# Identity products that nobody reads, in the last stage of a two-layer gated cross-attention kernel

## The chip, the cores and the metric

The kernel runs on one core of a Trainium2 chip. The metric is the device time of one execution, in microseconds. Before the change three runs gave 2161.19, 2162.99 and 2169.70 us, so the median is 2162.99 us.

## What is computed

The reference runs two layers over 32 sequences of 100 tokens with 128 features and a context of 1444 rows each. Layer 0 is a gated cross-attention block and a gated feed-forward with quantised weights. Layer 1 is a gated masked cross-attention with 16 heads of 8 and a gated feed-forward part, which is what the last stage of the kernel computes:

```python
attn_out = _attention(src, Wq, bq, Wk, bk, Wv, bv, Wo, bo)   # 16 heads over 100 tokens
x = _ln(src + attn_out, ln1_g, ln1_b)
ff = _moe(x, gW, gb, W1, b1, W2, b2)                         # 8 experts, width 256, top 2
return _ln(x + ff, ln2_g, ln2_b)
```

Every expert is computed for every token, and its hidden values are multiplied by the token's gate, which is zero for experts outside the top two. All of it is in fp32.

## The kernel before

The program has a setup and three stages, each in a block of its own: the engines meet at the border between two blocks. `stage_a` does layer 0, `stage_b` the masked cross-attention of layer 1, and `stage_c` (line 1646) all that follows. The change is in `stage_c`, in the stream of TensorE.

`stage_c` works on 8 units of 4 sequences (`UNITS`, `GROUP`), 400 tokens each (`TG`). The self-attention of a unit is cut into 8 pieces of half a sequence's heads, so there are 64 pieces (`PIECES`), and the order on every engine is written out as a loop over pieces k, one slot for each. In a slot TensorE issues, in this order:

- `scores(k + 1)` (line 2090): four heads' scores in each of two row groups of 32, into banks 0 and 1. They wait for `sub_ready`, VectorE's subtraction of the row maxima of piece k (lines 2316 and 2320), which frees these banks.
- `turn_pieces(k)` (line 2099): eight transposes of the exponentials. They wait for ScalarE's `exponent(k)` (line 1920).
- by the slot's place s in the unit's eight: a back-transpose of attended values (`back`, 2139), a turn of tokens (`turn0`, `turn1`, `turn2`, all through line 2038), or the query projection (2072).
- for slots from 22 on, `hidden(2n)` and `expert(2n - 2)` (lines 2191 and 2202), where n = k - 22.
- `weigh(k)` (line 2111): 16 heads' probabilities against values, eight matmuls of 32 columns of weights. It waits for ScalarE's copy of the transposed piece (`keep`, line 1926).
- again by s: the attended projection of the next unit (`attended`, 2053), the outer projection or values (through `project`, 2043), keys (2068), the gate's matmuls (2043).
- for slots from 22 on, `hidden(2n + 1)` and `expert(2n - 1)`.

The experts run 22 slots behind (`LAG`), because a unit's gates need the end of its attention. So slots 0 to 21 hold no expert work, slots 22 to 63 hold both, and 22 more steps (`TAIL`) hold the experts alone. Each `hidden` and `expert` is one matmul of 400 columns with 128 x 128 weights; GpSimd multiplies its hidden values by the gates in between (`weigh_hidden`, 1814), from a broadcast copy `G` that SyncE loads through DRAM (`spread_gates`, 1728).

Ahead of the slots stands a lead-in for unit 0: the attended projection, VectorE's entry with the moments of a layer norm (`enter`, 2304), GpSimd's reciprocal root, ScalarE's normalisation (1883), the turn, then keys, queries, values and the first scores, each waiting for ScalarE's copy of the one before (lines 1896, 1902, 1908).

PSUM bank 7 (`SUM_BANK`) holds the running sum of the experts; its first matmul is issued in slot 23 with `start=True`. At the end of `stage_a` there is already a helper `keep_busy` (line 863) of the same form as the new one, on bank 4.

Of the kernel before, what the change touches and what calls it, by code (L numbers as in the profile page):

```python
# [23 lines left out]
D = 128  # L24
# [5 lines left out]
TG = GROUP * T  # L30
# [1615 lines left out]
def stage_c(nc, t, x1, att, gates, w1, w2, out):  # L1646

    with ExitStack() as ctx:
# [6 lines left out]
        psum, K, tanhs, ident = t.psum, t.K, t.tanhs, t.ident  # L1655
        w, col, row, bank, tok_bank = t.w, t.col, t.row, t.bank, t.tok_bank
# [46 lines left out]
        OUT_BANK, MISC, HIDDEN_BANK, SUM_BANK = 4, 5, 6, 7  # L1703
# [10 lines left out]
        def sum_bank(u):  # L1714

            return OUT_BANK if u == LAST - 1 else SUM_BANK
# [316 lines left out]
        def _(pe):  # L2033
            mm = nc.tensor.matmul

            def turn(src, signal):
                for j in range(GROUP):
                    last = nc.tensor.transpose(bank(MISC, D, T, j * T), src[:, j, :], ident[0:T, 0:T])  # L2038
                last.then_inc(signal, 1)

            def project(b, lhsT, rhs, signal, width=D):
                for j in range(GROUP):
                    last = mm(bank(b, T, width, j * width), lhsT[:, t.ts_(j)], rhs, start=True, stop=True)  # L2043
                last.then_inc(signal, 1)

            def attended(u):
                pe.wait_ge(t.sem["ain_ready"], u + 1)
                if u == 1:
                    pe.wait_ge(sem["fv_ready"], 1)
                if u >= 2:  # L2050
                    pe.wait_ge(sem["fu_ready"], (u - 1) * GROUP)
                for j in range(GROUP):
                    m = mm(bank(MISC, T, D, j * D), AIN[:, u % 2, t.ts_(j)], w("xo"), start=True, stop=True)  # L2053
                m.then_inc(sem["attx_psum"], 1)

            def turn0(u):
                pe.wait_ge(normed[0], u + 1)
                if u == 1:
                    pe.wait_ge(sem["fu_ready"], 1)
                if u >= 2:  # L2060
                    pe.wait_ge(sem["r_used"], u - 1)
                turn(H[:, u % 3], turned[0])

            def keys(u):
                pe.wait_ge(tokT[0], u + 1)
                if u:
                    pe.wait_ge(sem["fu_ready"], (u - 1) * GROUP + 2)
                mm(bank(MISC, D, TG), w("fk"), HT[:, :], start=True, stop=True).then_inc(sem["fk_psum"], 1)  # L2068

            def queries(u):  # L2070
                pe.wait_ge(sem["fk_ready"], u + 1)
                mm(bank(MISC, D, TG), w("fq"), HT[:, :], start=True, stop=True).then_inc(sem["fq_psum"], 1)  # L2072

            def values(u):
                pe.wait_ge(sem["fq_ready"], u + 1)
                if u:
                    pe.wait_ge(sem["fu_ready"], (u - 1) * GROUP + 3)
                project(MISC, HT, w("fv"), sem["fv_psum"])

            def scores(k):  # L2080
                m, c = divmod(k, 2)
                u, j = divmod(m, GROUP)
                pe.wait_ge(sem["kbd_ready"], m + 1)
                pe.wait_ge(sem["fq_ready"], u + 1)
                if k:
                    pe.wait_ge(sem["sub_ready"], k)
                for b in range(2):
                    r = 2 * c + b
                    dims = slice(32 * r, 32 * r + 32)
                    x_ = mm(bank(b, T, TG), FQ[dims, u % 2, t.ts_(j)], KBD[dims, u % 2, j, :],  # L2090
                            start=True, stop=True, tile_position=(32 * r, 0))
                x_.then_inc(sem["fs_psum"], 1)

            def turn_pieces(k):
                pe.wait_ge(sem["fe_ready"], k + 1)
                if k:
                    pe.wait_ge(sem["fpT_ready"], k)
                for a in range(8):
                    x_ = nc.tensor.transpose(bank(2 + a // 4, T, T, (a % 4) * T), P[:, k % 2, t.ts_(a)], ident[0:T, 0:T])  # L2099
                x_.then_inc(sem["fpT_psum"], 1)  # L2100

            def weigh(k):
                m, c = divmod(k, 2)
                u, j = divmod(m, GROUP)
                pe.wait_ge(sem["fpT_ready"], k + 1)
                pe.wait_ge(sem["fv_ready"], u + 1)
                if m and not c:
                    pe.wait_ge(sem["os_ready"], m)
                for a in range(8):
                    r, q = a % 4, 2 * c + a // 4  # L2110
                    x_ = mm(psum[32 * r:32 * r + 32, OUT_BANK, q * T:(q + 1) * T], VS[:, u % 2, j, 8 * c + a, :],  # L2111
                            PT[:, k % 2, a // 4, t.ts_(r)], start=True, stop=True, tile_position=(0, 32 * r), skip_group_check=True)
                x_.then_inc(sem["fo_psum"], 1)
# [28 lines left out]
            def turn1(u):  # L2142
                pe.wait_ge(sem["fu_ready"], (u + 1) * GROUP)
                if u + 2 < UNITS:
                    pe.wait_ge(sem["x_ready"], u + 3)
                turn(U[:, u % 2], turned[1])

            def outer(u):
                pe.wait_ge(tokT[1], u + 1)
                pe.wait_ge(sem["fu_ready"], min((u + 1) * GROUP + 1, BATCH))  # L2150
                project(MISC, OT, w("fo"), sem["wo_psum"])

            def turn2(u):
                pe.wait_ge(sem["y_ready"], u + 1)
                if u + 2 < UNITS:
                    pe.wait_ge(sem["fv_ready"], u + 3)
                elif u < LAST:
                    pe.wait_ge(sem["fu_ready"], LAST * GROUP + 3)
                else:
                    pe.wait_ge(sem["u_ready"], LAST - 2)  # L2160
                turn(Y[:, u], turned[2])
# [32 lines left out]
            def expert(c):  # L2194
                u, w_ = divmod(c, 2 * EXPERTS)
                b = bank(sum_bank(u), D, TG)
                if w_ == 0 and u:
                    pe.wait_ge(sem["yT_ready"], u)
                if w_ == 0 and u == LAST - 1:
                    pe.wait_ge(sem["os_ready"], BATCH)  # L2200
                pe.wait_ge(sem["moe_g_ready"], c + 1)
                mm(b, W2[:, w_ * D:(w_ + 1) * D], HE[:, c // 2 % 2, c % 2, :], start=(w_ == 0), stop=False,  # L2202
                   skip_group_check=True).then_inc(sem["moe_y_psum"], 1)
                if w_ == 2 * EXPERTS - 1:
                    pe.wait_ge(g_loaded[0], 32 * (u + 1))
                    mm(b, t.B2[:, :], WT[:, u % 2, :], start=False, stop=True, skip_group_check=True).then_inc(sem["yT_psum"], 1)

            attended(0)
            turn0(0)
            keys(0)  # L2210
            queries(0)
            values(0)
            scores(0)
            for k in range(PIECES):
                b, s = divmod(k, SLOTS)
                n = k - LAG
                if k + 1 < PIECES:
                    scores(k + 1)
                turn_pieces(k)
                if s % 2 == 0 and k:  # L2220
                    back(k // 2 - 1)
                if s == 1 and b:
                    turn1(b - 1)
                if s == 3 and b < LAST:
                    turn0(b + 1)
                if s == 5 and b < LAST:
                    queries(b + 1)
                if s == 7 and b:
                    turn2(b - 1)
                if n == 0:  # L2230
                    pe.wait_ge(sem["big_loaded"], 32)
                if n >= 0:
                    hidden(2 * n)
                if n >= 1:
                    expert(2 * n - 2)
                weigh(k)
                if s == 0 and b < LAST:
                    attended(b + 1)
                if s == 2 and b:
                    outer(b - 1)  # L2240
                if s == 4 and b < LAST:
                    keys(b + 1)
                if s == 5 and b >= 4:
                    turn_experts(b - 4)
                if s == 6 and b < LAST:
                    values(b + 1)
                if s == 7 and b:
                    gate(b - 1)
                if n >= 0:
                    hidden(2 * n + 1)  # L2250
                if n >= 1:
                    expert(2 * n - 1)
# [262 lines left out]
```

## Time and profile before

| what | value |
|---|---|
| median of 3 runs | 2162.99 us |
| profiled execution | 2172.06 us, span 2170.3 us |
| TensorE busy | 1935.4 us, 89% of the span |
| VectorE, ScalarE, GpSimd busy | 68%, 61%, 31% |
| mean granted clock of TensorE | 0.924 |
| last stage | from 1675.46 us to the end of the span |

A granted clock of 1.00 is 2.4 GHz and 0.50 is 1.2 GHz; a figure in between is a stretch with both. The profile has one row for a group of equal instructions that follow each other: start, time from the first start to the last end, engine, line, the tensors written and read, shapes, count. An fp32 matmul leaves two records, so a single product of 400 columns reads x2. "Idle before" in brackets is the wait of that engine and what ended it.

### The profile page before, as it was taken

What the parts mean: (1) busy time and instruction counts of PE and PEld (TensorE: products, weight loads), DVE (VectorE), ACT (ScalarE), POOL (GpSimd) and SP (SyncE); (2) the same over time, 40 slices, a digit from 0 to 9 for tenths busy, and PEclk for the clock granted to TensorE, in tenths of its full rate; (3) what the DMA queues carried; (4) which work ended last, traced back from release to release, by engine and by line L of the source; (5) the groups of instructions that cost most, each with busy time, mean ns of one, the idle gap of its engine ahead of it and who ended that gap; (6) DMA issues with size and microseconds to landing.
All of it is one profiled execution on the core that took longest, in us unless ns stands there. A gap on an engine that the chain in (4) does not pass through costs nothing. (4 is left out here: it accounts for less than half of the span.)

```text
span 2170.3 us, 42902 instructions
## 1 busy us (share of the span) xinstructions
PE 1935.4 (89%) x16792; PEld 1224.2 (56%) x16792; DVE 1481.8 (68%) x3509; ACT 1321.2 (61%) x2169; POOL 670.7 (31%) x605
## 2 busy tenths in 40 slices
PE   3669999766899999999999999999998899999997
PEld 2536766444465656656566565665655455555553
DVE  4844666785778787777877778777783456577541
ACT  2635677586166666666666666666776345666643
POOL 1410223321422131322313223131221323566576
PEclk9879999877599999999999999999999557999998
DMA  5025555001232332323323232232332102221222
GB/s 157 1 69 189 168 186 172 26 27 47 89 106 82 114 119 72 131 82 114 108 84 131 81 115 97 95 131 68 124 105 75 24 12 45 48 41 36 36 70 42
DMA packets 126293, 190.74 MB, mean 88 GB/s; under 512 B 42018, under 2 KB 99466, under 8 KB 125710
## 3 DMA queue, kind: packets, MB, share of 16 engines
q1 hardware_dynamic: 126094, 188.01, 27.9%
q8 instruction: 134, 2.20, 0.4%
q14 instruction: 65, 0.53, 0.1%
HBM read 104.84 MB, written 11.76 MB: 54 GB/s over the span
## 5 line engine op out<-in xcount | busy, mean ns | idle before, releaser
L1607 DVE TENSOR_REDUCE b_part_max<-psum 128x1 f32<-128x482 f32 (+3 forms) x1248 | 738.6, 650 | 200.8 <-PE psum L1493 186.0
L1413 ACT ACTIVATE b_PT<-psum 128x800 f32<-128x800 f32 x768 | 614.9, 836 | 335.4 <-PE psum L1512 329.5
L1493 PE MATMUL psum<-b_KH,b_QBD 64*128 64x482 f32 (+1 forms) x1152 | 416.2, 441 | 37.4 <-DVE b_part_max L1607 35.0
L1512 PE MATMUL psum<-b_QS,b_KS 64*128 64x200 f32 x3072 | 436.7, 288 | 0.3 <-ACT b_PT L1413 0.3
L1512 PEld LDWEIGHTS psum<-b_QS,b_KS 64*128 64x128 f32 x3072 | 346.2, 187 | 15.2 <-issue 10.5
L1528 PE MATMUL psum<-b_PT,b_V 128*32 128x200 f32 x6144 | 341.4, 339 | 0.3 <-ACT b_PT L1413 0.3
L1493 PEld LDWEIGHTS psum<-b_KH,b_QBD 64*128 64x128 f32 x1152 | 194.1, 189 | 182.1 <-DVE b_part_max L1607 115.7
L1338 POOL TENSOR_TENSOR b_KL<-b_KF,b_KH 128x1444 fp32r<-128x1444 f32 x32 | 106.9, 3340 | 589.7 <-PE psum L1512 566.5
L1528 PEld LDWEIGHTS psum<-b_PT,b_V 128*32 128x32 f32 x6144 | 159.9, 109 | 144.6 <-ACT b_PT L1413 78.7
L1814 POOL TENSOR_TENSOR c_HE<-c_HE,c_G 128x400 f32<-128x400 f32 x128 | 131.5, 1032 | 112.6 <-ACT c_HE L1960 106.0
L426 POOL TENSOR_TENSOR a_rs<-a_ve,a_half 100x4 f32<-100x4 f32 x48 | 48.5, 1011 | 312.6 <-DVE a_ve L918 312.5
L2316 DVE TENSOR_REDUCE c_peak<-psum 100x8 f32<-100x800 f32 x64 | 63.2, 987 | 96.0 <-PE psum L2090 95.9
L1480 PE MATMUL psum<-W,b_CT 128*128 128x128 f32 (+1 forms) x768 | 117.7, 293 | 7.0
L1960 ACT ACTIVATE c_HE<-psum,C 128x400 f32<-128x400 f32 x128 | 75.5, 593 | 75.9 <-PE psum L2191 74.7
L2202 PE MATMUL psum<-c_HE,c_W 128*128 128x400 f32 x256 | 110.1, 513 | 9.7 <-POOL c_HE L1814 9.3
L1480 PEld LDWEIGHTS psum<-W,b_CT 128*128 128x128 f32 (+1 forms) x768 | 92.7, 188 | 35.5 <-DVE b_part_max L1607 31.6
L1926 ACT COPY c_PT<-psum 100x800 f32<-100x800 f32 x64 | 52.8, 825 | 96.6 <-PE psum L2099 96.6
L2191 PE MATMUL psum<-c_YT,c_W 128*128 128x400 f32 x256 | 110.4, 513 | 0.0
L1476 PE MATMUL psum<-b_CT,W 128*128 128x482 f32 (+1 forms) x192 | 103.0, 623 | 6.5 <-DVE b_QF L1589 2.5
L959 DVE TENSOR_SCALAR_CACHE_REDUCE a_nz<-psum 1x422 bf16<-1x422 f32 (+1 forms) x96 | 59.8, 643 | 67.4 <-PE psum L716 67.3
L716 PE MATMUL psum<-a_CT,a_RT 128*100 128x422 f32 (+1 forms) x192 | 93.0, 596 | 8.3 <-ACT a_P L524 7.1
L741 PE MATMUL psum<-a_P,a_CN 128*128 128x100 f32 (+1 forms) x768 | 98.9, 281 | 0.0
(280 smaller groups left out, 2988.2 us busy)
## 6 DMA issues: line engine op xcount, KB each, us to landing
b_KS<-b_KH SPq DMA_DIRECT2D x64, 722.0 KB
a_CT<-in_ctxt SPq DMA_DIRECT2D x32, 722.0 KB, 5.6
b_CT<-in_ctxt SPq DMA_DIRECT2D x32, 722.0 KB, 4.3
b_KS<-b_KL SPq DMA_DIRECT2D x32, 722.0 KB
a_CN<-in_ctxn SPq DMA_DIRECT2D x32, 704.0 KB
c_G<-gates_scratch SPq DMA_DIRECT2D x16, 800.0 KB, 4.3
att_scratch<-b_AO SPq DMA_DIRECT2D x32, 200.0 KB, 5.8
b_MB<-in_mask SPq DMA_DIRECT2D x32, 180.5 KB, 4.4
```

The lines of the kernel that those rows point to most:

```text
L741: x_ = mm(bank(7, D, T, TG), CN[0:rows, m % 3, k, :], PTA[0:rows, m % 2, k, :], start=(k == 0), stop=(k == KT - 1))
L1338: pl.tensor_tensor(KL[:, :], KF[:, 0:S], KH[:, j % 2, :].bitcast(F32), ALU.subtract).then_inc(sem["kl_ready"], 1)
L1413: nc.scalar.activation(PT[:, kt % 2, 2 * a:2 * a + 2, :], psum[:, 2 * a:2 * a + 2, 0:TG], ACT.Exp).then_inc(sem["pt_ready"], 1)
L1476: m = mm(bank(b, D, size), w("xkT"), CT[:, j % 2, c:c + size], start=True, stop=True)
L1480: m = mm(bank(b, rows, D, (k % 4) * D), CT[:, j % 2, k * D:k * D + rows], w("xvT"), start=True, stop=True)
L1493: m = mm(bank(b, D, size), QBD[rows, j % 2, tile * D:(tile + 1) * D], KH[rows, j % 2, at_:at_ + size], start=True, stop=True)
L1512: m = mm(bank(p, D, 2 * T, (s % 2) * 2 * T), KS[rows, j % 2, s, kt * D:(kt + 1) * D], QS[rows, j % 2, s * 2 * T:(s + 1) * 2 * T], start=Tr ...
L1528: m = mm(psum[32 * r:32 * r + 32, 6, b * 2 * T:(b + 1) * 2 * T], V[:, j % 2, kt, 4 * b + r, :], PT[:, kt % 2, 2 * b + r // 2, (r % 2) * 2 ...
L1607: v.tensor_reduce(part_max[0:rows, q, c:c + 1], bank(b, rows, CHUNKS[c][1]), AX.X, ALU.max)\
L1814: pl.tensor_tensor(h, h, G[:, e, :], ALU.mult).then_inc(sem["moe_g_ready"], 1)
L2191: mm(bank(hidden_bank(c), D, TG), W1[:, w_ * D:(w_ + 1) * D], YT[:, u, :], start=True, stop=True).then_inc(sem["moe_h_psum"], 1)
L2202: mm(b, W2[:, w_ * D:(w_ + 1) * D], HE[:, c // 2 % 2, c % 2, :], start=(w_ == 0), stop=False, skip_group_check=True).then_inc(sem["moe_y_p ...
```

## The change

A helper `keep_busy(count)` issues `count` matmuls: the 128 x 128 identity as weights, the first 400 columns of the weight pack `W` as the moving operand, into bank 7. It waits for nothing and signals nobody, and nobody reads the result. In the lead-in there are six products ahead of `attended(0)`, three ahead of `turn0(0)`, and two ahead of each of `keys(0)`, `queries(0)`, `values(0)` and `scores(0)`. In each slot with n < 0 (slots 0 to 21) two stand ahead of `turn_pieces(k)` and two ahead of `weigh(k)`. That is 17 + 88 = 105 products.

```diff
--- before.py
+++ after.py
@@ -2205,17 +2205,30 @@
                     pe.wait_ge(g_loaded[0], 32 * (u + 1))
                     mm(b, t.B2[:, :], WT[:, u % 2, :], start=False, stop=True, skip_group_check=True).then_inc(sem["yT_psum"], 1)
 
+            def keep_busy(count):
+
+                for _ in range(count):
+                    mm(bank(SUM_BANK, D, TG), ident, t.W[:, 0:TG], start=True, stop=True)
+
+            keep_busy(6)
             attended(0)
+            keep_busy(3)
             turn0(0)
+            keep_busy(2)
             keys(0)
+            keep_busy(2)
             queries(0)
+            keep_busy(2)
             values(0)
+            keep_busy(2)
             scores(0)
             for k in range(PIECES):
                 b, s = divmod(k, SLOTS)
                 n = k - LAG
                 if k + 1 < PIECES:
                     scores(k + 1)
+                if n < 0:
+                    keep_busy(2)
                 turn_pieces(k)
                 if s % 2 == 0 and k:
                     back(k // 2 - 1)
@@ -2233,6 +2246,8 @@
                     hidden(2 * n)
                 if n >= 1:
                     expert(2 * n - 2)
+                if n < 0:
+                    keep_busy(2)
                 weigh(k)
                 if s == 0 and b < LAST:
                     attended(b + 1)
```

The change moves no other instruction. On TensorE, in the lead-in of the last stage (W is the weight pack, K holds the identity, c_H, c_HT, c_P and c_PT are the normalised tokens, the same turned, the exponentials and the same turned), the order was:

```order
L2053 MATMUL psum<-W,AIN 100x128 x4
L2038 MATMUL psum<-K,c_H 128x100 x4
L2068 MATMUL psum<-c_HT,W 128x400
L2072 MATMUL psum<-c_HT,W 128x400
L2043 MATMUL psum<-W,c_HT 100x128 x4
L2090 MATMUL psum<-c_KBD,c_FQ 100x400 x4
L2099 MATMUL psum<-K,c_P 100x100 x8
L2111 MATMUL psum<-c_PT,c_VS 32x100 x8
```

and is now, with line 2211 the new product:

```order
L2211 MATMUL psum<-W,K 128x400 x6
L2053 MATMUL psum<-W,AIN 100x128 x4
L2211 MATMUL psum<-W,K 128x400 x3
L2038 MATMUL psum<-K,c_H 128x100 x4
L2211 MATMUL psum<-W,K 128x400 x2
L2068 MATMUL psum<-c_HT,W 128x400
L2211 MATMUL psum<-W,K 128x400 x2
L2072 MATMUL psum<-c_HT,W 128x400
L2211 MATMUL psum<-W,K 128x400 x2
L2043 MATMUL psum<-W,c_HT 100x128 x4
L2211 MATMUL psum<-W,K 128x400 x2
L2090 MATMUL psum<-c_KBD,c_FQ 100x400 x4
```

Each real step of the lead-in has products ahead of it, six of them ahead of the first; the row of four score matmuls is pieces 0 and 1 together.

On TensorE in slots 1 and 2, the order was:

```order
L2090 MATMUL psum<-c_KBD,c_FQ 100x400 x2
L2099 MATMUL psum<-K,c_P 100x100 x8
L2111 MATMUL psum<-c_PT,c_VS 32x100 x8
L2090 MATMUL psum<-c_KBD,c_FQ 100x400 x2
L2099 MATMUL psum<-K,c_P 100x100 x8
L2139 MATMUL psum<-K,c_OS 100x128 x4
L2111 MATMUL psum<-c_PT,c_VS 32x100 x8
```

and is now:

```order
L2090 MATMUL psum<-c_KBD,c_FQ 100x400 x2
L2211 MATMUL psum<-W,K 128x400 x2
L2099 MATMUL psum<-K,c_P 100x100 x8
L2211 MATMUL psum<-W,K 128x400 x2
L2111 MATMUL psum<-c_PT,c_VS 32x100 x8
L2090 MATMUL psum<-c_KBD,c_FQ 100x400 x2
L2211 MATMUL psum<-W,K 128x400 x2
L2099 MATMUL psum<-K,c_P 100x100 x8
```

A pair of products now stands between scores and transposes, and another between transposes and weighting; none stands between the weighting and the next scores.

## Rows read from the trace of the kernel before

**Rows 1.** The page, 40 equal slices of the span: TensorE's granted clock in tenths.

```profile
PEclk9879999877599999999999999999999557999998
```

**Rows 2.** Windows of the last stage: busy us (count) by engine, granted clock, DMA share, GB/s.

```profile
1675.46:1695.08 19.62, 9.48 (x28) 4.96 (x29) 5.05 (x18) 4.02 (x9) 11.93 (x11) 0.51 0.42 140
1695.08:1819.80 124.72, 117.40 (x757) 72.35 (x757) 72.48 (x182) 54.31 (x90) 27.30 (x26) 0.54 0.11 16
1819.80:1833.63 13.83, 11.40 (x96) 6.64 (x92) 7.14 (x13) 7.49 (x13) 7.68 (x10) 1.00 0.40 121
1833.63:1882.22 48.59, 48.59 (x356) 27.82 (x355) 29.49 (x86) 30.06 (x54) 30.32 (x30) 1.00 0.26 48
```

**Rows 3.** Timeline of the lead-in: start us, us, engine, line, tensors, shapes, count [idle before].

```profile
1675.46 1.53 PE L2053 MATMUL psum<-W,AIN 128*100 128x128 f32 x8 [2.99 <-PEq L1173]
...
1677.59 0.75 DVE L2307 SCALAR_TENSOR_TENSOR c_X<-psum,tanhs,XIN 100x512 f32<-100x512 f32 x1 [1.45 <-POOL XIN L1774]
...
1682.90 0.93 PE L2038 MATMUL psum<-K,c_H 100*128 100x100 f32 x4 [5.91 <-ACT c_H L1883]
...
1684.41 1.70 PE L2068 MATMUL psum<-c_HT,W 128*128 128x400 f32 x2 [0.58 <-ACT c_HT L1896]
...
1691.15 1.66 PE L2090 MATMUL psum<-c_KBD,c_FQ 32*100 32x400 f32 x4
...
1695.08 1.66 PE L2090 MATMUL psum<-c_KBD,c_FQ 32*100 32x400 f32 x4 [2.27 <-DVE c_P L2320]
```

**Rows 4.** Timeline, TensorE: score matmuls of two neighbouring slots at half clock.

```profile
1706.84 1.66 PE L2090 MATMUL psum<-c_KBD,c_FQ 32*100 32x400 f32 x4
...
1711.74 1.66 PE L2090 MATMUL psum<-c_KBD,c_FQ 32*100 32x400 f32 x4
```

**Rows 5.** Timeline, TensorE: an expert slot, and the start of slot 30.

```profile
1839.96 0.92 PE L2090 MATMUL psum<-c_KBD,c_FQ 32*100 32x400 f32 x4
1840.81 0.89 PE L2099 MATMUL psum<-K,c_P 100*100 100x100 f32 x8
1841.54 0.51 PE L2038 MATMUL psum<-K,c_U 100*128 100x100 f32 x4
1841.88 0.86 PE L2191 MATMUL psum<-c_YT,c_W 128*128 128x400 f32 x2
...
1843.35 0.55 PE L2111 MATMUL psum<-c_PT,c_VS 100*32 100x100 f32 x16
1843.83 0.94 PE L2191 MATMUL psum<-c_YT,c_W 128*128 128x400 f32 x2
...
1845.37 0.92 PE L2090 MATMUL psum<-c_KBD,c_FQ 32*100 32x400 f32 x4
...
1869.09 0.92 PE L2090 MATMUL psum<-c_KBD,c_FQ 32*100 32x400 f32 x4
```

**Rows 6.** Timeline, TensorE: two score matmuls in a stretch at full clock, without experts.

```profile
1758.40 0.92 PE L2090 MATMUL psum<-c_KBD,c_FQ 32*100 32x400 f32 x4
...
1762.85 0.92 PE L2090 MATMUL psum<-c_KBD,c_FQ 32*100 32x400 f32 x4 [1.24 <-DVE c_P L2320]
```

**Rows 7.** Timeline, TensorE: the first stage's own identity products, with the turn before them.

```profile
534.17 0.57 PE L647 MATMUL psum<-K,a_U 100*128 100x100 f32 x4 [3.35 <-ACT a_U L475]
534.58 3.55 PE L867 MATMUL psum<-W,K 128*128 128x400 f32 x10
```

**Rows 8.** Windows of one microsecond: the clock falling at the border, falling and returning later.

```profile
1675.00:1676.00 1.00, 0.54 (x5) 0.56 (x6) 0.53 (x3) 0.00 (x0) 0.10 (x1) 0.98 0.00 0
2099.00:2100.00 1.00, 1.00 (x4) 0.50 (x3) 0.00 (x0) 0.00 (x0) 1.00 (x2) 0.61 0.85 346
2102.00:2103.00 1.00, 1.00 (x7) 0.85 (x6) 0.00 (x0) 0.17 (x1) 0.80 (x1) 0.69 0.60 109
```

**Rows 9.** Timeline, TensorE: the score matmul of slot 19 and the first expert product.

```profile
1805.23 1.66 PE L2090 MATMUL psum<-c_KBD,c_FQ 32*100 32x400 f32 x4
...
1830.03 0.94 PE L2202 MATMUL psum<-c_HE,c_W 128*128 128x400 f32 x2 [2.08 <-POOL c_HE L1814]
```

## The prediction

> **What bounds the kernel now.** I read the page's forty slices first. The granted clock there is high nearly everywhere except, late in the run, in the slices around 1,700 to 1,820 us, the start of the last stage [rows 1]. The windows then cut the stage by its own marks [rows 2]: the lead-in (19.62 us, TensorE busy 9.48), the 22 slots without experts (124.72 us, busy 117.40, granted clock 0.54), the joint where the experts start (13.83 us), and one full batch of eight slots with experts (48.59 us, all of them busy, clock 1.00). So the 22 slots are bound by TensorE, but by a TensorE at 1.2 GHz; a slot with experts holds about 3 us more matmuls and is hardly longer, because it runs at 2.4 GHz. The question is what is left of that difference once identity products fill it.
>
> A plain slot at half clock lasts 4.90 us from one score matmul to the next [rows 4]. Where the clock came back for a few microseconds, a slot with a turn of tokens took 4.45 us, and 1.24 us of that was a wait for VectorE's subtraction [rows 6]. At full clock and unfilled, then, the softmax chain between the engines is near. At full clock and filled, TensorE's own work is longer than that chain: the expert slot from 1839.96 to 1845.37 has no idle time in it [rows 5].
>
> **The change, part by part.**
>
> *Price of a product.* The first stage holds the same instruction: ten records, which are five products, in 3.55 us at full clock [rows 7], 0.69 us each once the last one's tail of some 0.1 us is off. In a slot the neighbours have other shapes and cost a little at each seam: the pair of expert matmuls ahead of the weighting takes 1.47 us (1841.88 to 1843.35), the pair behind it 1.54 (1843.83 to 1845.37) [rows 5]. I take 1.46 us for a filling pair: a filled slot holds two, 2.92, an expert slot two at 3.0. At half clock a pair would be near twice that, 2.9 us. The Trainium skill ("TensorE: Matmul & The Clock Gate", Back-to-back issue gap) gives N/2.4 plus 2.5 ns between isolated matmuls, about 0.17 us for 400 columns as an estimate; the trace disagrees for these fp32 operands, by the row just named. By that rule the sum would be up to 49 us smaller (rival C).
>
> *The 22 slots.* If the clock is full, a filled slot costs what the expert slot at the same place of the batch costs. The batch of eight is 48.59 us [rows 2]; it holds one bias matmul of the experts, about 0.7 us, so 47.9. Slots 0 to 7 lack what has no batch before them: a back-transpose 0.44, two turns of 0.34, the outer projection 0.95, the gate 0.73 (steps between starts in that batch): 45.1. Slots 8 to 15 are whole: 47.9. Slots 16 to 21 are the first six, 1833.63 to 1869.09 [rows 2, 5]: 35.5. Together 128.5, less 0.08 for each of 22 slots: 126.7 us. Counting only TensorE's pieces (scores 0.85, transposes 0.73, weighting 0.48 [rows 5], the projections, and products of 0.68) gives 123.2. Against 124.72 now that is +2.0, with bounds of −1.5 and +3.8. The filling costs what the clock gives: 88 products of 0.73 us are 64 us of new work, and the doubled clock and the covered waits remove about 62. I see no new wait: between a score matmul and the next TensorE has 4.1 us of work, and VectorE's maximum and subtraction need 2.3 [rows 3].
>
> *The lead-in.* The stage opens with the attended projection, 1675.46 to 1676.99; VectorE starts on it at 1677.59, having waited for GpSimd [rows 3]. Six products now stand ahead of it. The clock falls just then, after 2.99 us of idle at the stage's border (0.98 in the microsecond from 1675, half afterwards [rows 2, 8]). Where it fell late in the stage with 400-column matmuls queued, it was back after some 3.4 us [rows 8]. So: 0.5 us full, 3.4 us half, the rest full. Six products are 4.2 us of full-clock work; 2.2 are done when the clock returns near 1679.4, the last 2.0 end near 1681.4, the projection near 1682.4. VectorE starts at 1682.5 in place of 1677.59: +4.9. The three products ahead of the turn stand in its wait of 5.91 us [rows 3] and cost nothing; without that cover they would cost 2.1. From the turn to the second score matmul (12.18 us now [rows 3]) the pairs are longer than the waits they stand in (0.58 ahead of the keys, the others alike), the one ahead of the first scores stands in none, and the full clock shortens the real matmuls: turn 0.34, four pairs 5.84, keys and queries 0.76 each, values 0.95, then 3.2 for scores, maximum and subtraction; 11.9 together, −0.3. Lead-in: +4.6. One thing is open: between the projection and the turn TensorE still idles some 3.3 us. The first stage kept its clock over 3.35 us of idle [rows 7], the stage's border lost it over 2.99. I count half of a second fall, which would cost 1.7: +0.9. Bounds for the lead-in: +3 (the clock never falls) and +8.
>
> *The joint.* Expert 0's first product waits 2.08 us for GpSimd, which waits for the broadcast gates; from the score matmul at 1805.23 to that product are 24.8 us [rows 9]. Filled slots 19 to 21 take 17.2 us, slot 22 with two hidden products 4.9, and 2.6 lie ahead of the expert's: TensorE arrives after 24.6 us. The gates come about 1 us sooner than now, since the scores that VectorE works on first are quicker. The wait closes, and 13.83 us [rows 2] become about 11.5: −2.3, bounds −2.8 and 0.
>
> *Sum.* +2.0 +4.6 +0.9 −2.3 = +5.2 us. Nothing behind the joint changes: the expert slots are busy throughout and already at full clock. The profiled execution took 2172.06 us, so 2177.3 by its level; the median of the runs is 2162.99, 9 lower, which gives 2168.2. Part of that distance may lie in this very stage: a run in which the clock comes back oftener in the unfilled slots is quicker, and the filled kernel has nothing of that to gain. I put 2 us on it: **2170**.
>
> **The rivals.**
>
> *A: clearly slower.* The clock does not stay up in the filled slots. For it: TensorE is busy 94% of the 22 slots now and is not granted full speed, so busy time alone does not bring it [rows 2]. Against: a filled slot holds the same two pairs as an expert slot, at 1.00 for 48 us, and the same products ran at full speed in the first stage [rows 7]. Price: at half clock a filled slot is 4.90 less 1 us of waits plus 5.8, so 9.7, 4.7 more than at full clock. Two such slots pass the 10.8 us that count as slower; five give 2193, all 22 some 2273. The Trainium skill ("TensorE: Matmul & The Clock Gate", Part 4) says that full clock does not engage for transposes; if products against an identity matrix counted the same way, this rival would be the outcome. No run here shows the two apart.
>
> *B: the forecast's mechanism, worse sizes.* Two falls in the lead-in, seams as dear as in expert slots, a joint that closes little: +8 +3.8 −0.5, so +11: 2174 to 2181.
>
> *C: faster.* Each product lies in a wait and costs almost nothing beyond it; then every slot would be near the unfilled 4.45 us at full clock [rows 6], 98 us for 22 of them, 27 less than now: 2141. The row of five products in 3.55 us speaks against it: two pairs are longer than any wait in a slot. This is where the skill's issue gap, named above, would lead.
>
> *D: the instructions are added but TensorE skips ahead of them or they vanish.* The order of the instructions shows them in place, and TensorE's queue runs in order; the time would be 2163.
>
> **How the numbers follow.** A measurement of this kernel can tell about 0.5%, 10.8 us, from no change. Forecast, +1 to +10: 0.66. B: 0.20. A: 0.07. C: 0.02. D or a sum between −10 and +1: 0.05. B lies half on either side of +10.8, and the question of the level may carry the forecast's upper end over it (0.09). That makes faster 0.04 with a lucky comparison, same 0.70, slower 0.26. The range takes the forecast and most of B: 2160 to 2181.
>
> **What would show it.** Granted clock 0.95 or more in the 22 slots, their window near 127 us; filled slots of 5.0 to 6.4 us with no idle time; VectorE's first step on the projection 4 to 6 us later than now; the wait ahead of the first expert product gone. Wrong would be: clock 0.5 in filled slots, a filled slot under 4.7 us, or waits for VectorE or ScalarE still ahead of scores or weighting.

## The result and the profile after

The changed kernel took 2185.37 us (median of 4 runs, 2182.83 to 2192.76) beside 2162.09 us (4 runs, 2160.93 to 2169.70) for the kernel before: a ratio of 1.009, interval 1.0061 to 1.0119 (the two medians alone are 23.3 us, or 1.1%, apart). It is slower by 0.9% by the ratio, and its median lies 4 us above the upper end of the range given. Its profiled execution took 2186.38 us, with a span of 2184.6 and a mean granted clock of 0.946, up from 0.924. TensorE's clock is better and the time is worse.

The page of the changed kernel, the granted clock in 40 slices:

```profile
PEclk8879999877599999999999999999999999999997
```

Beside [rows 1], the low slices late in the run are gone. The windows of its last stage are the lead-in, the 22 slots without experts, the joint, the 38 slots with both, and all behind the last score matmul (busy us and count by engine, granted clock, DMA share, GB/s):

```profile
1675.63:1701.98 26.35, 20.75 (x63) 11.58 (x63) 5.05 (x18) 4.03 (x9) 11.93 (x11) 0.81 0.32 104
1701.98:1831.02 129.04, 129.04 (x933) 75.27 (x933) 72.44 (x182) 55.67 (x90) 29.38 (x28) 0.99 0.11 16
1831.02:1842.51 11.49, 11.14 (x97) 6.75 (x93) 6.91 (x13) 6.89 (x12) 7.16 (x9) 1.00 0.40 145
1842.51:2073.88 231.37, 228.92 (x1673) 130.83 (x1672) 151.37 (x439) 145.43 (x255) 140.17 (x135) 1.00 0.22 38
2073.88:2184.60 110.72, 91.17 (x317) 48.01 (x316) 32.64 (x128) 43.69 (x87) 70.51 (x67) 0.86 0.25 55
```

The first three answer to [rows 2]: the lead-in went from 19.62 to 26.35 us, the slots from 124.72 to 129.04 with TensorE busy in all of it and the clock at 0.99, and the joint from 13.83 to 11.49. The fourth is level (231.39 before). The fifth was 105.28 us in the profiled execution before (from 2065.02 us to the end of the span), 5.4 us shorter, though the change touches nothing in it. These five parts are what the experiments are read by. The timeline of the lead-in, beside [rows 3] (start, us, engine, line, tensors, shapes, count, idle before):

```profile
1675.63 5.96 PE L2211 MATMUL psum<-W,K 128*128 128x400 f32 x12 [2.98 <-PEq L1173]
1681.43 1.04 PE L2053 MATMUL psum<-W,AIN 128*100 128x128 f32 x8
...
1682.50 0.75 DVE L2322 SCALAR_TENSOR_TENSOR c_X<-psum,tanhs,XIN 100x512 f32<-100x512 f32 x1 [6.20 <-PE psum L2053]
...
1687.81 0.93 PE L2038 MATMUL psum<-K,c_H 100*128 100x100 f32 x4 [3.33 <-ACT c_H L1883]
...
1701.98 0.92 PE L2090 MATMUL psum<-c_KBD,c_FQ 32*100 32x400 f32 x4 [2.27 <-DVE c_P L2335]
```

VectorE starts at 1682.50. The clock is down by the end of the idle stretch of 3.33 us ahead of the turn, and it falls again within 2 us behind the 2.27 us of idle ahead of the second scores, as windows of one microsecond show:

```profile
1687.00:1688.00 1.00, 0.19 (x1) 0.19 (x2) 0.00 (x0) 0.76 (x2) 1.00 (x1) 0.50 0.19 36
...
1705.00:1706.00 1.00, 1.00 (x9) 1.00 (x7) 0.01 (x1) 0.00 (x0) 0.00 (x0) 0.50 0.00 0
```

### The profile page after: what moved, and what is told of

The parts are those of the page before. It is cut to its first block and busy times, and to the rows that moved or that the text cites. A ratio compares the mean times of both kernels' runs of the same rounds, so it can differ in the third digit from the quotient of the medians.

```text
span 2184.6 us, 43322 instructions
## 1 busy us (share of the span) xinstructions
PE 1968.4 (90%) x17002; PEld 1241.0 (57%) x17002; DVE 1480.9 (68%) x3509; ACT 1322.1 (61%) x2169; POOL 670.6 (31%) x605
```

## Experiments

Every kernel here computes all of the reference's outputs. The kernels of a group ran on one chip, beside runs of the kernel before on that chip, whose medians were 2171.52 us (35 runs, 2156.89 to 2184.56) for the first four, 2170.94 (23 runs, 2159.14 to 2183.89) for the next four, and 2168.59 (30 runs, 2158.51 to 2187.49) for the last four. The kernel before differs by up to 29 us between its own executions within one group.

### What part costs what

*The kernel before again,* nothing edited.

> The kernel before, unchanged, for a second profile and for how far its runs lie apart. Theory 1 (run-to-run luck of the clock): the first profiled execution, 2172 us, had an unlucky clock in the 22 slots without experts; an execution near 2162 us shows these slots in 113 to 120 us in place of 124.7, with more than 7 us of full clock among them, and nothing else moved by over 2 us. Theory 2 (the luck lies in the tail or in the first stage): the 22 slots stay at 124 to 126 us and the 9 us lie before 542 us or after 2076 us. Time: same as before, ratio within 0.3% of 1.

Measured 2170.46 us (12 runs, 2160.85 to 2183.92), 0.9999 of before (0.9973 to 1.0024). Its profiled execution took 2160.96 us. The windows of its lead-in, its 22 slots, its joint, and what lies behind its last score matmul:

```profile
1674.51:1694.11 19.60, 9.45 (x28) 4.91 (x29) 5.05 (x18) 4.02 (x9) 11.91 (x11) 0.51 0.44 140
1694.11:1808.61 114.50, 102.52 (x756) 62.81 (x756) 72.20 (x182) 54.56 (x89) 28.66 (x28) 0.65 0.13 17
1808.61:1820.10 11.49, 11.21 (x96) 6.74 (x93) 6.90 (x13) 7.76 (x14) 7.80 (x9) 1.00 0.39 145
2051.48:2159.10 107.62, 88.08 (x317) 46.81 (x316) 32.65 (x128) 43.68 (x87) 70.54 (x67) 0.89 0.25 56
```

The same unfilled slots took 114.50 us here and 124.72 in [rows 2]; what differs is the clock, 0.65 against 0.54. The joint was 11.49 with nothing added. Its TensorE timeline in one of the good stretches:

```profile
1741.63 0.92 PE L2090 MATMUL psum<-c_KBD,c_FQ 32*100 32x400 f32 x4
1742.48 0.89 PE L2099 MATMUL psum<-K,c_P 100*100 100x100 f32 x8
...
1746.15 1.14 PE L2090 MATMUL psum<-c_KBD,c_FQ 32*100 32x400 f32 x4 [1.31 <-DVE c_P L2320]
1747.22 1.57 PE L2099 MATMUL psum<-K,c_P 100*100 100x100 f32 x8
```

The clock was high for the slot from 1741.63 and gone again by 1747.22, where the same eight transposes take 1.57 us in place of 0.89. How often it comes back in the unfilled slots differs between executions in which nothing was edited; below this is called a draw. Between these two it is worth 10 us.

*The changed kernel again,* nothing edited, in the first and in the third group.

> The changed kernel, unchanged, for a second profile. Theory 1: lead-in and 22 slots are the same to 2 us (full clock nearly everywhere), the last 100 us after the slots differ by several us from the first profile, as the clock falls after other waits. Theory 2: the tail is again 99 to 100 us, 5 us over that of before, in every execution of the filled kernel. Time 2182 to 2190.

> The changed kernel a third time. Theory 1 (a draw): its tail after the last score matmul, 110.7 us in both profiles, is now between 105 and 111 like that of the others; lead-in 26.3 and slots 129.0 again to 1.7 us. Rival (filling moves the tail into a worse place against the clock in every run): 110.7 again. Time 2182 to 2189.

Measured 2186.59 us (12 runs, 2177.78 to 2194.62), 1.0071 of before (1.0041 to 1.0101); and 2183.65 us (12 runs, 2178.05 to 2192.59), 1.0072 (1.0045 to 1.0098). By means of the runs it is 16.1 us slower both times. The first of the two profiles repeats the parts of the first profile after, the end included, which had been expected to differ; the second has a cheaper lead-in and end (its windows, and its turn of tokens in the lead-in):

```profile
1674.66:1698.16 23.50, 17.88 (x63) 10.08 (x63) 5.06 (x18) 4.03 (x9) 11.94 (x11) 0.93 0.35 116
1698.16:1827.20 129.04, 129.04 (x932) 75.00 (x932) 72.52 (x182) 55.76 (x90) 29.38 (x28) 0.99 0.11 16
2070.13:2176.30 106.17, 86.55 (x317) 46.11 (x316) 32.65 (x128) 43.77 (x87) 70.62 (x67) 0.91 0.27 57
```

```profile
1686.86 0.56 PE L2038 MATMUL psum<-K,c_H 100*128 100x100 f32 x4 [3.34 <-ACT c_H L1883]
```

The filled slots are not drawn: 129.04 us in all three, to 0.02. The lead-in is (26.35, 26.28, 23.50): in the third profile the clock stayed up over the 3.34 us ahead of the turn, which took 0.56 us, while the same wait of 3.33 us in the first profile after was followed by a turn of 0.93 us at half clock. The end behind the last scores is drawn too (110.72, 110.75, 106.17).

*The slots alone,* and *the lead-in alone.* First the 17 products of the lead-in out of the changed kernel, then the 88 of the slots:

```diff
-            keep_busy(6)
             attended(0)
-            keep_busy(3)
             turn0(0)
-            keep_busy(2)
             keys(0)
-            keep_busy(2)
             queries(0)
-            keep_busy(2)
             values(0)
-            keep_busy(2)
             scores(0)
```

> The 88 products of the 22 slots alone, none in the lead-in. Theory 1 (the parts add up as the trace has them: lead-in +7, slots +4.3, joint -2.3): 7 us less than the changed kernel, 2176 to 2180. Rival (the slots carry the loss, since unfilled slots in a median run have more full clock than the profile showed): 2180 to 2184, the lead-in's products give only 2 to 4 us.

```diff
                     scores(k + 1)
-                if n < 0:
-                    keep_busy(2)
                 turn_pieces(k)
...
                     expert(2 * n - 2)
-                if n < 0:
-                    keep_busy(2)
                 weigh(k)
```

> The 17 products of the lead-in alone; the 22 slots as before. Theory 1: +6 to +7 us over before for the lead-in, less what a full clock at the start of the slots gives back (0 to 3 us): 2165 to 2170. Rival: full clock at the start of the slots keeps itself up without filling; then the slots shrink from 124.7 towards 100 us and the time is under 2150.

Slots alone: 2176.25 us (12 runs, 2173.77 to 2184.44), 1.0039 of before (1.0011 to 1.0066). Lead-in alone: 2173.83 us (12 runs, 2164.70 to 2183.36), 1.0004 (0.9976 to 1.0032). The window of the 22 slots of the first:

```profile
1696.01:1825.62 129.61, 129.61 (x933) 75.01 (x933) 72.46 (x182) 55.67 (x90) 29.38 (x28) 0.98 0.11 15
```

and the windows of the lead-in and of the 22 slots of the second:

```profile
1680.31:1703.79 23.48, 17.88 (x63) 10.07 (x63) 5.05 (x18) 4.02 (x9) 11.92 (x11) 0.93 0.36 117
1703.79:1821.85 118.06, 105.21 (x757) 64.46 (x757) 72.19 (x182) 55.12 (x90) 29.05 (x28) 0.63 0.12 17
```

The slots alone cost 0.39%, 7 us by the means of the runs: filled slots at 129.61, joint 11.49. The second kernel gives a third draw of unfilled slots, 118.06, though one that starts with the clock up. Its joint was 13.79, with TensorE busy in all of it at a clock of 0.79, where the 13.83 of [rows 2] held idle time at a clock of 1.00. The lead-in alone adds 3.9 us in its window; its timed runs can't be told from before, and its median is above the 2165 to 2170 expected because that of before is. The two ratios add up to 0.43% and both parts together cost 0.71%; with intervals of 0.3% each way the runs don't show whether that is more than their sum.

*Without the six products ahead of the attended projection,* all else as changed:

```diff
-            keep_busy(6)
             attended(0)
             keep_busy(3)
             turn0(0)
```

> The changed kernel without the six products at the head of the lead-in. The prediction's term: they cost 4.9 us. Theory 1: lead-in 21 to 22.5 us in place of 26.3, time 4 to 5 us under the changed kernel, 2181 to 2183 beside a kernel before near 2171. Rival (the six buy a full clock that the rest of the lead-in needs): lead-in 24 to 26 us, time unchanged to 2 us.

Measured 2180.55 us (12 runs, 2174.95 to 2183.83), 1.0040 of before (1.0022 to 1.0059). The window of its lead-in:

```profile
1674.75:1695.07 20.32, 15.40 (x50) 9.01 (x51) 5.05 (x18) 4.02 (x9) 11.93 (x11) 0.83 0.40 135
```

That is 20.32 us, 6.0 less than 26.35, and in both the turn ran at half clock (0.93 us). VectorE starts 2.13 us after the lead-in does, as before, where it was 6.87 with the six: 4.7 of the 6.0 us. The lead-in is 0.7 us above the unfilled one, so the other eleven products cost next to nothing. The six stand where nothing hides them: their output is not read, but the projection behind them is what VectorE, GpSimd and ScalarE wait for.

### Where a product stands, and how many

The slots alone still lose, so the filling is too dear for what the clock gives. Three kernels halve it: no products in the lead-in, and 44 in place of 88 in the slots. *One at each place,* *the pair ahead of the transposes only,* and *the pair ahead of the weighting only*; the lead-in as in the slots-only kernel, and against the changed kernel:

```diff
                 if n < 0:
-                    keep_busy(2)
+                    keep_busy(1)
                 turn_pieces(k)
...
                 if n < 0:
-                    keep_busy(2)
+                    keep_busy(1)
                 weigh(k)
```

> Half the filling: one product at each of the two places of a slot, none in the lead-in. Theory 1 (TensorE-bound when filled, the price is the products' own time): if one and one still hold the full clock, a slot is 4.8 less 1.4, so 3.4 us of matmuls plus projections and some waits; the 22 slots take 95 to 105 us in place of 129.6 with two and two and of 114 to 125 unfilled, and the time is 2148 to 2158. Theory 2 (two pairs are needed): the clock falls in most slots, a slot at half clock with one and one is near 7.5 us, and the time is 2185 or more.

```diff
                     expert(2 * n - 2)
-                if n < 0:
-                    keep_busy(2)
                 weigh(k)
```

> Only the pair ahead of the transposes in each slot, none in the lead-in. The same number of products as one and one. Theory 1: the time is that of one and one to 3 us if the clock sees only how much stands in a slot, but TensorE's wait of about 1 us for ScalarE's copy stays uncovered ahead of the weighting: 0.5 us more for each slot, +5 to +11 us over one and one. Theory 2: clock falls, 2185 or more.

```diff
                     scores(k + 1)
-                if n < 0:
-                    keep_busy(2)
                 turn_pieces(k)
```

> Only the pair ahead of the weighting in each slot, none in the lead-in. Theory 1: it covers the wait for ScalarE's copy and leaves the one for VectorE's subtraction; within 3 us of one and one. Theory 2: clock falls in most slots, 2185 or more.

| 44 products in the slots | median us | runs | of before (interval) | 22 slots us |
|---|---|---|---|---|
| one and one | 2156.35 | 6 | 0.9934 (0.9914 to 0.9955) | 104.81 |
| pair ahead of transposes | 2162.28 | 12 | 0.9975 (0.9952 to 0.9997) | 114.79 |
| pair ahead of weighting | 2152.68 | 6 | 0.9919 (0.9897 to 0.9942) | 103.57 |

The windows of the 22 slots with one and one, and then with the pair ahead of the transposes (its waits follow: what was waited for, us in total, times, longest):

```profile
1703.15:1807.96 104.81, 100.80 (x844) 58.83 (x844) 71.55 (x182) 54.94 (x90) 27.96 (x27) 0.98 0.13 19
1694.93:1809.72 114.79, 103.20 (x845) 61.33 (x845) 72.29 (x182) 54.07 (x90) 28.34 (x27) 0.96 0.12 17
```

Its waits there:

```profile
PE psum L2111 <- ACT c_PT L1926: 11.6, 22, 0.9
```

The same two with the pair ahead of the weighting:

```profile
1695.18:1798.75 103.57, 99.28 (x845) 58.85 (x845) 71.52 (x182) 56.63 (x90) 27.91 (x27) 0.98 0.13 19
```

```profile
PE psum L2090 <- DVE c_P L2327: 5.4, 6, 2.3
```

Both have the clock, 0.96 and 0.98, with half the products. In the first TensorE waits ahead of the weighting in every slot, 11.6 us in all, for ScalarE's copy of the transposed piece: the pair delays the transposes, and with them the copy. In the second the pair stands in that very wait, and the listed wait is gone; a shorter one, for VectorE's subtraction, is left. Of the 11.2 us between the two kernels, 7.3 are idle time (11.59 against 4.29) and 3.9 are busy time, at a clock of 0.96 against 0.98. A slot of each from the timelines; first, ahead of the transposes:

```profile
1732.13 0.92 PE L2090 MATMUL psum<-c_KBD,c_FQ 32*100 32x400 f32 x4
1732.97 1.61 PE L2211 MATMUL psum<-W,K 128*128 128x400 f32 x4
...
1736.19 0.55 PE L2111 MATMUL psum<-c_PT,c_VS 100*32 100x100 f32 x16 [0.92 <-ACT c_PT L1926]
1736.67 0.92 PE L2090 MATMUL psum<-c_KBD,c_FQ 32*100 32x400 f32 x4
```

Then a slot with no extra piece (slots without a back-transpose or projection) with the pair ahead of the weighting:

```profile
1728.44 0.92 PE L2090 MATMUL psum<-c_KBD,c_FQ 32*100 32x400 f32 x4
...
1730.02 1.53 PE L2211 MATMUL psum<-W,K 128*128 128x400 f32 x4
1731.48 0.55 PE L2111 MATMUL psum<-c_PT,c_VS 100*32 100x100 f32 x16
1731.96 0.92 PE L2090 MATMUL psum<-c_KBD,c_FQ 32*100 32x400 f32 x4
```

3.52 us for the slot here and 4.54 in the kernel above, where 0.92 is the wait. Such a slot with both pairs takes 4.93 us in the changed kernel, from 1709.62 to 1714.55 (shown below). The pair ahead of the transposes, 1.45 us there, accounts for the 1.41 us between 4.93 and 3.52.

### From the best dose onwards

Four kernels on one chip, the changed kernel's third profile (told above) among them. The other three start from the pair ahead of the weighting. *A single product there:*

```diff
                 if n < 0:
-                    keep_busy(2)
+                    keep_busy(1)
                 weigh(k)
```

> One product a slot, ahead of the weighting. Theory 1 (the dose still suffices): the 22 slots are bound by the chain over VectorE and ScalarE, 97 to 103 us, time 0 to 5 us under the pair's. Rival (too little): clock falls in some of the plain slots, the 22 slots take 106 to 116 us and the time is 5 us or more above the pair's, between the pair and the kernel before.

Measured 2147.92 us (9 runs, 2146.81 to 2163.22), 0.9919 of before (0.9884 to 0.9955). The windows of its 22 slots and of its joint:

```profile
1697.25:1796.07 98.82, 89.80 (x801) 53.54 (x801) 71.56 (x182) 55.59 (x90) 27.34 (x26) 0.92 0.14 20
1796.07:1810.52 14.45, 12.44 (x97) 6.90 (x93) 7.15 (x13) 7.99 (x14) 8.69 (x10) 0.93 0.31 114
```

Even 22 products hold the clock at 0.92. The slots shrink by another 4.7 us and the joint, which was 11.5 with the pair, gives back 3, with 2.0 us of idle time in it and a clock of 0.93. Its ratio is that of the pair.

*The pair, and products in the three longest waits for GpSimd behind the last score matmul,* into bank 6, between `hidden(2n + 1)` and `expert(2n - 1)` of the last 22 steps, numbered i:

```diff
                 hidden(2 * n + 1)
+                if i in (5, 14, 21):
+                    keep_busy(3 if i == 5 else 2, HIDDEN_BANK)
                 expert(2 * n - 1)
```

> The pair ahead of the weighting in slots 0 to 21, and besides seven products in the three waits for GpSimd of the last 22 steps (three in 2.88 us, two in each 1.94 us; into the idle bank 6). Theory 1 (the tail's 105 to 111 us are a draw of how often the clock falls after these waits, 1.7 us each): the tail takes 103.5 to 104.5 us in every execution, the spread of the runs shrinks, and the time is 2 to 5 us under the pair alone. Rival (the falls come from elsewhere, or the products delay the experts): tail 105 us or more, time unchanged or +2.

Measured 2149.43 us (10 runs, 2144.71 to 2159.21), 0.9921 of before (0.9889 to 0.9952). The window behind its last scores:

```profile
2041.41:2144.20 102.79, 87.52 (x331) 47.23 (x330) 33.27 (x128) 43.77 (x87) 70.55 (x67) 0.96 0.27 59
```

The timeline at the longest wait as it is now, three products and the rest of the wait:

```profile
2071.82 2.18 PE L2211 MATMUL psum<-W,K 128*128 128x400 f32 x6
2074.88 0.94 PE L2202 MATMUL psum<-c_HE,c_W 128*128 128x400 f32 x2 [0.88 <-POOL c_HE L1814]
```

What is drawn in this end of the stage is seen at the same wait in kernels that leave it empty. The expert product behind it in the changed kernel, with a window of the six microseconds from 2107:

```profile
2107.34 1.70 PE L2202 MATMUL psum<-c_HE,c_W 128*128 128x400 f32 x2 [2.89 <-POOL c_HE L1814]
```

```profile
2107.00:2113.00 6.00, 5.66 (x12) 3.25 (x13) 0.98 (x1) 1.09 (x2) 4.27 (x5) 0.50 0.71 234
```

the same product in the profiled execution of the kernel before:

```profile
2098.48 1.01 PE L2202 MATMUL psum<-c_HE,c_W 128*128 128x400 f32 x2 [2.88 <-POOL c_HE L1814]
```

and in the third profile of the changed kernel:

```profile
2103.60 0.94 PE L2202 MATMUL psum<-c_HE,c_W 128*128 128x400 f32 x2 [2.89 <-POOL c_HE L1814]
```

The waits are equal, the outcomes are three. In the first the clock was down before the product started and stayed down for over six microseconds. In the second it fell while the product ran and was back within four: that is the fall of [rows 8], at 2099 and 2102. In the third it did not fall here at all. Leaving out the last 21 us, the 14 profiles sort by the falls in their end: two long ones give 110.7 us (three profiles), two short ones 107.6 to 107.9 (three), one short one 105.3 to 106.2 (six), none 102.8 and 103.5. So a short fall costs some 2 us here. The 102.79 us with the waits filled, at a clock of 0.96, are the shortest; but the 103.54 are an execution with the waits empty (the single product ahead of the weighting), so one profile does not show that the filling made it so. The timed runs don't separate this kernel from the pair alone, and they spread over 14.5 us, beside 7.6 to 16.4 for the other kernels of the smaller doses: the spread that was to shrink did not.

*The pair, and six products in the lead-in where they delay no projection:* three in the wait ahead of the turn, three behind the first scores.

```diff
             attended(0)
+            keep_busy(3)
             turn0(0)
             keys(0)
             queries(0)
             values(0)
             scores(0)
+            keep_busy(3)
```

> The pair ahead of the weighting, and in the lead-in only products that stand in long waits: three ahead of the turn (wait 5.9 us) and three behind the first scores (wait 2.3 us). Theory 1 (products in a longer wait are free, and the clock they bring helps what follows): lead-in 17 to 19.6 us, slot 0 about 1 us shorter, 1 to 4 us less than the pair alone. Rival: the clock falls again behind them, lead-in unchanged at 19.6, nothing gained; or the three behind the scores at half clock (4 us) outlast their wait, +1 to +2 us.

Measured 2151.93 us (12 runs, 2146.44 to 2160.64), 0.9917 of before (0.9890 to 0.9944). The window of its lead-in:

```profile
1685.09:1706.38 21.29, 16.69 (x41) 8.46 (x41) 5.06 (x18) 4.78 (x9) 11.91 (x11) 0.60 0.40 129
```

The three products behind the first scores, in its timeline:

```profile
1702.35 4.09 PE L2211 MATMUL psum<-W,K 128*128 128x400 f32 x6
```

At half clock the three last 4.09 us, longer than the wait of 2.27 they stand in: 1.7 us lost there, and 2.3 won in the slots (101.25 against 103.57), which start with the clock up. The three ahead of the turn gained nothing, since the clock was down again for the turn, as without them. Nothing is left of it in the timed runs.

This profile shows one more draw. Its execution took 2158.01 us, 9.4 more than the profiled one of the pair alone, and the last stage starts 9.5 us later in it (1685.09 against 1675.57): the difference lies ahead of everything that the change touches. Over the 14 profiles that start lies between 1672.80 and 1685.09 us. In the two latest of them, this one and one and one, the first stage was granted 0.86 between 300 and 450 us, where the other twelve had 0.91 or 0.92 there.

These kernels beat both: the pair or the single product ahead of the weighting, with nothing in the lead-in, is 0.8% faster than before, 18 and 21 us by the medians of their groups. The single product is 33 us faster than the change as made, by the means of the same group.

## Why the prediction was wrong

The forecast was 2170 us, no measurable difference; the kernel is 0.7 to 0.9% slower. The mechanism was right: full clock in the filled slots, TensorE busy in all of them, VectorE's start late, the wait ahead of the experts closed. Two things were not: what the unfilled slots cost, against which the filled ones were set, and the level of the kernel before.

**Filled slots: right in kind, 2 us short.** The prediction gave 126.7 us at full clock with no idle time; measured 129.04, all of it busy. The TensorE timeline of slots 0 and 1 shows both the price of a pair and the missing 2 us:

```profile
1702.82 2.02 PE L2211 MATMUL psum<-W,K 128*128 128x400 f32 x4
...
1709.62 0.92 PE L2090 MATMUL psum<-c_KBD,c_FQ 32*100 32x400 f32 x4
1710.47 1.61 PE L2211 MATMUL psum<-W,K 128*128 128x400 f32 x4
1711.92 0.85 PE L2099 MATMUL psum<-K,c_P 100*100 100x100 f32 x8
1712.61 1.53 PE L2211 MATMUL psum<-W,K 128*128 128x400 f32 x4
1714.07 0.55 PE L2111 MATMUL psum<-c_PT,c_VS 100*32 100x100 f32 x16
1714.55 0.92 PE L2090 MATMUL psum<-c_KBD,c_FQ 32*100 32x400 f32 x4
```

A pair takes 1.45 us ahead of the transposes (1710.47 to 1711.92) and 1.46 ahead of the weighting (1712.61 to 1714.07), as taken from [rows 5, 7]. Slot 0, from 1701.98 to 1709.62, took 7.64 us: the clock fell in it, behind the 2.27 us of idle time. By the steps of slot 1 and an attended projection of 1.04 us it would be 6.0 at full clock, as an estimate, so 1.7 of the missing 2.3 us are this fall. The issue gap in the Trainium skill ("TensorE: Matmul & The Clock Gate", Back-to-back issue gap) would give 0.17 us for one of these fp32 products, as an estimate; the trace shows over four times that. The Trainium skill also says that full clock does not engage for transposes (the same page, Part 4); the filled slots, with transposes and products against an identity matrix in them, ran at 0.99, which does not tell what the transposes count for.

**Unfilled slots: the step that failed.** The prediction set the 126.7 us "against 124.72 now" and called it +2.0. It took one execution's 124.72 for what these slots cost. Three executions draw 124.72, 114.50 and 118.06, in mean 119.1; the filled slots have no draw. So the term is +9.9 us, though three draws that spread over 10 us leave that mean uncertain by some 3 us. The closing of the joint failed the same way: the joint did come down to 11.49, the 11.5 forecast, but unfilled slots gave 13.83, 11.49 and 13.79, so −2.3 is −1.5. The prediction named the effect ("a run in which the clock comes back oftener in the unfilled slots is quicker, and the filled kernel has nothing of that to gain") and put 2 us on it. It is some 6 us, 5.6 in the slots and 0.8 in the joint; with the 2.3 by which the filled slots are dearer that makes 8.7. The slots-only kernel bears this out by its runs: +0.39% (0.11 to 0.66), where the prediction's terms for slots and joint come to −0.3 us.

**The level: the other step that failed.** With 2172.06 for the profiled execution and 2162.99 for a median of three, the prediction went most of the way to the lower one. In 88 later runs of the kernel before the medians of the groups were 2168.6 to 2171.5. The three runs were a low draw, the profiled execution an ordinary one. From its level the same sum of +5.2 gives 2177, still inside the range. From a middle median of 2170.5, with the slots 7.9 us and the joint 0.8 us dearer as told above, the sum is +13.9, and the time 2184: neither error alone carries it past 2181.

**The lead-in: right in kind, in size partly by luck.** VectorE's start was forecast at 1682.5 and was 1682.50; counted from the start of the lead-in it moved by 4.7 us (+4.9 forecast). The window came out at 26.35, 26.28 and 23.50 us, a mean of 25.4, against 19.6: +5.8, where +4.6 and half of a second fall (+0.9) made +5.5. But without the second fall it was +3.9 in place of +4.6, and the fall, which came in two of three profiles, costs 2.8 us in place of 1.7: the errors cancel.

**Nothing behind the joint: right for what the change moves, and blind to a draw.** The 38 slots took 231.37 us in place of 231.39. The end behind them drew 105.28 and 107.62 in the two profiles of before and 107.86 with the lead-in alone, and 110.72, 110.75 and 106.17 with the change: +2.3 in mean. With the slots alone it was 105.70, without the six products 106.24, with one and one 110.74. These lengths follow the number and length of the clock's falls, as told above. So the changed kernel can have a short end too; whether the change makes the long one more frequent is left open.

Together: +5.8 lead-in, +9.9 slots, −1.5 joint, +2.3 end are +16.5 us by the means of the profiles (three of the change; two of before and, but for the lead-in, the lead-in-alone kernel); the timed runs give +16.1, twice. That the two agree so closely is in part luck: the sum leaves out what lies ahead of the last stage, which started 2.4 us earlier in mean in the three profiles of the change than in the other three.

**The rivals.** A, a clock that stays low in filled slots, is excluded by 0.99 over the 22 slots. B came nearest in size, with the two falls in the lead-in that it names, but its seams were not dear and its joint closed fully. C named the wrong place: two pairs don't hide. A smaller dose does: the prediction priced the filling only as it stood, though it had worked out 98 us for 22 slots from the 4.45 us of [rows 6], and 22 products come to 98.82.

## What to carry to other kernels

Work that only keeps the clock up pays while it fits into the waits that it stands in; beyond that it is ordinary work, and each microsecond of it is paid for. Start with the smallest dose, place it in a wait (here ahead of the weighting, behind the transposes that ScalarE is waiting for), and not ahead of an instruction that other engines wait for. Where the granted clock of a stretch is in between its two levels, one execution is one draw: take several profiles of the kernel before, and its level from many runs, before setting a change of 1% against it.

## What the hardware showed that was not expected

- One product of 0.69 us in a slot of some 4.5 us, 22 in all, went with a granted clock of 0.92, where the three profiles with unfilled slots had 0.54 to 0.65. In the first profile before, TensorE was busy for 94% of the same slots; with the single products it was busy for 91% (89.80 of 98.82 us). The busier slots had the lower clock. Part of that is the clock's own doing, since eight transposes that take 0.89 us at full clock keep TensorE busy for 1.57 at half; no run here isolates what brought the clock back.
- Waits of the same length had either outcome, in one and the same kernel: in the changed kernel's lead-in the clock was down after 3.33 us of idle in one execution and up after 3.34 in another, and the wait of 2.89 us near the end did the same (2107.34 and 2103.60 in their profiles). The first stage of the kernel before kept it over 3.35 us [rows 7].
- A fall near the end of the stage lasted under four microseconds in some executions and over six in others, and the number and length of the falls there set this end's length between 102.8 and 110.8 us in 14 profiles.
- The same 44 products in the same slots gave 103.57, 104.81 or 114.79 us by where they stood, a wider spread than between 22 products and 44 at the best place (98.82 and 103.57).
